# Self-attention's output projection by three float32r products of high and low parts, in a decoder layer on one core

## The reference

```
x = x + attn(layernorm(x))          # 16 heads of 128, one shared key/value head, rotary, causal
x = x + xattn(layernorm(x), ctx)    # 16 heads of 16 over 1500 context rows, layernorm of the output
x = x + ffn(layernorm(x))           # gated, with quantised activations and ternary weights
```

```
out = jnp.einsum('bhij,bjd->bhid', attn, v)
out = out.transpose(0, 2, 1, 3).reshape(b, n, h * dh)
return out @ Wo                     # (.., 2048) @ (2048, 256)
```

## Time and profile before

| | |
|---|---|
| median of 3 runs | 1477.72 us |
| the profiled execution's own time | 1479.29 us |
| its span, first to last instruction | 1477.5 us |
| PE busy | 1376.1 us, 93% |
| DVE busy | 1009.2 us, 68% |
| ACT busy | 717.3 us, 49% |
| POOL busy | 442.2 us, 30% |
| L643 records on PE | 512, 114.1 us busy |
| mean granted TensorE clock | 0.970 of full speed |

### The profile page before, as it was taken

The page is one execution under the profiler, slowest core; times in us unless marked ns, Lnnn a source line. Parts: engine busy times, 40 slices in busy tenths (PEclk is TensorE's granted clock), DMA queues, the critical chain, the costliest instruction groups (busy, mean ns, idle before and its releaser), DMA issues.

```text
span 1477.5 us, 55098 instructions
## 1 busy us (share of the span) xinstructions
PE 1376.1 (93%) x25094; PEld 1176.1 (80%) x25094; DVE 1009.2 (68%) x1786; ACT 717.3 (49%) x939; POOL 442.2 (30%) x394
## 2 busy tenths in 40 slices
PE   3899999999299999999999999999999999999983
PEld 3687777786278888888888888888888888888871
DVE  4666666765044686877778687876877777677765
ACT  1444454443155555464555555555555555555540
POOL 2332232231032323333333333332323233232400
PEclk8899999999689999999999999999999999999995
DMA  7000000000422211212121121211112121111100
GB/s 210 1 2 25 5 1 29 1 2 1 107 58 58 56 50 45 61 31 75 48 59 48 44 62 31 75 50 57 48 44 61 30 76 59 47 48 44 48 6 3
DMA packets 38809, 66.75 MB, mean 45 GB/s; under 512 B 3605, under 2 KB 36818, under 8 KB 38578
## 3 DMA queue, kind: packets, MB, share of 16 engines
q1 hardware_dynamic: 38578, 63.24, 14.7%
HBM read 61.40 MB, written 1.84 MB: 43 GB/s over the span
## 4 chain that ended last, share of the span: by engine, by line
PE 68%; DVE 3%; issue 1%; POOL 0%; POOLq 0%; DVEq 0%
PE proj_ps L1196 19%; PE proj_ps L1187 18%; PE score_ps L1214 13%; PE sum_ps L1234 12%; PE side_ps L1265 3%; PE side_ps L1251 2%; PE side_ps L1279 1%; PE side_ps L1272 1%; PE side_ps L1258 0%; DVE amax L1072 0%; DVE exps L1019 0%; DVE inv L1031 0%; POOL low L894 0%; DVE vals L1010 0%; DVE hidden L1104 0%
## 5 line engine op out<-in xcount | busy, mean ns | idle before, releaser
L954 ACT ACTIVATE exps<-score_ps 125x1792 f32<-125x1792 f32 x192 | 320.6, 1670 | 418.8 <-PE score_ps L1214 418.8
L894 POOL TENSOR_TENSOR low<-raw,high 128x500 fp32r<-128x500 f32 x192 | 293.6, 1537 | 645.1 <-PE proj_ps L1187 510.3
L1019 DVE TENSOR_SCALAR exps<-exps,top 125x896 f32<-125x896 f32 x384 | 288.1, 792 | 18.0 <-ACT exps L954 17.5
L1214 PE MATMUL score_ps<-spread,keys 32*125 32x112 f32 x6144 | 218.9, 279 | 0.9 <-ACT exps L954 0.9
L1234 PEld LDWEIGHTS sum_ps<-exps,vals 125*32 125x32 f32 x12288 | 163.5, 110 | 47.6 <-issue 33.9
L1214 PEld LDWEIGHTS score_ps<-spread,keys 32*125 32x125 f32 x6144 | 184.8, 183 | 16.3 <-ACT exps L954 1.0
L1010 DVE COPY vals<-proj_ps 125x512 f32<-125x512 f32 x192 | 128.3, 688 | 96.8 <-PE proj_ps L1196 96.3
L1234 PE MATMUL sum_ps<-exps,vals 125*32 125x56 f32 x12288 | 192.0, 215 | 0.1
L1196 PE MATMUL proj_ps<-w_h,high 128*125 128x256 f32 x768 | 165.0, 296 | 0.0
L1187 PE MATMUL proj_ps<-high,w_h 128*128 128x500 f32 x384 | 132.8, 427 | 25.4 <-POOL low L894 25.4
L946 ACT ACTIVATE keys<-proj_ps,b_k 128x500 f32<-128x500 f32 x192 | 130.0, 677 | 52.4 <-PE proj_ps L1187 48.0
(11 more groups left out here) (129 smaller groups left out, 1668.2 us busy)
## 6 DMA issues: line engine op xcount, KB each, us to landing
raw<-in_ctxT SPq DMA_DIRECT2D x96, 500.0 KB, 3.7
w_q<-in_attn_Wq SPq DMA_DIRECT2D x4, 512.0 KB, 6.7
w_o<-in_attn_Wo SPq DMA_DIRECT2D x1, 2048.0 KB, 19.9
out<-y_out SPq DMA_DIRECT2D x16, 112.0 KB, 2.0
rows<-in_x SPq DMA_DIRECT2D x1, 1568.0 KB, 14.8
w_raw<-in_ffn_gate_wT SPq DMA_DIRECT2D x1, 1024.0 KB, 8.6
w_raw<-in_ffn_val_wT SPq DMA_DIRECT2D x1, 1024.0 KB, 5.0
w_raw<-in_ffn_out_wT SPq DMA_DIRECT2D x1, 1024.0 KB, 5.8
```

Source lines behind the costliest of these rows:

```text
L894: nc.gpsimd.tensor_tensor(low[r][:, k, :], raw[ring][:, k, :], high[r][:, k, :].bitcast(F32), ALU.subtract).then_inc(low_ready, 1)
L954: nc.scalar.activation(exps[t % 2][:, :, :, :].rearrange("p h r n -> p r h n"), score_ps[0:TILE, :, 0:2 * QW].rearrange("p r (h n) -> p r ...
L1019: nc.vector.tensor_scalar(tile, tile, LIMIT_LO, top[:, n, at:at + 1], ALU.max, ALU.min)\
L1214: ins = nc.tensor.matmul(score_ps[0:TILE, r, to:to + HE * S], keys[c % 2][32 * r:32 * r + 32, k, (at + half) * TILE:(at + half + 1) * TILE ...
```

## The change

`Wo` and the heads' outputs are each split in two: a high part, which is the value rounded to float32r by a copy on ScalarE, and a low part, which is the value less its high part, computed on VectorE. The projection becomes three float32r matmuls per head (high with high, high with low, low with high) in place of one float32 matmul.

- `Wo` is split once, in pair 0: four ScalarE copies of 128x1024 after `exps(0)`, four VectorE subtractions of 128x1024 after the third rotary step.
- The heads' outputs are split in every pair: ScalarE's four copies write `outT_h` as float32r, and VectorE gets four new subtractions `out_low` of 128x448, each reading `out_ps` and `outT_h`. Two stand after the third rotary step and two after the fourth. `outT_ready`, for which `out_heads` and `out_rows` wait, is now counted by VectorE's subtractions and no longer by ScalarE's copies.
- `outT` had two buffers, `outT_h` and `outT_l` have one each.

```diff
@@ DVE
+            def out_low(p, k, b):
+                dve.wait_ge(outT_high, 2 * (2 * p + k) + b + 1)
+                nc.vector.tensor_tensor(outT_l[:, AU * k:AU * (k + 1), b * S:(b + 1) * S],
+                                        out_ps[:, b, 0:AU * S].rearrange("p (h s) -> p h s", s=S),
+                                        outT_h[:, AU * k:AU * (k + 1), b * S:(b + 1) * S].bitcast(F32),
+                                        ALU.subtract).then_inc(outT_ready, 1)
+            def out_weights(n):
+                dve.wait_ge(w_o_high, n + 1)
+                nc.vector.tensor_tensor(w_ol[:, 4 * n:4 * n + 4, :], w_o[:, 4 * n:4 * n + 4, :],
+                                        w_oh[:, 4 * n:4 * n + 4, :].bitcast(F32), ALU.subtract).then_inc(w_o_split, 1)
...
                 for name in more[2:3]:
                     rotary(name)
+                for n in range(4) if p == 0 else ():
+                    out_weights(n)
+                for b in range(2):
+                    out_low(p, 0, b)
                 if p:
                     norm2_rows(p - 1)
                 for name in more[3:4]:
                     rotary(name)
+                for b in range(2):
+                    out_low(p, 1, b)
@@ ACT
             def out_half(p, k, b):
                 act.wait_ge(pv_done, 2 * p + k + 1)
-                ins = nc.scalar.copy(outT[p % 2][:, AU * k:AU * (k + 1), b * S:(b + 1) * S],
-                                     out_ps[:, b, 0:AU * S].rearrange("p (h s) -> p h s", s=S))
-                ins.then_inc(outT_ready, 1)
+                nc.scalar.copy(outT_h[:, AU * k:AU * (k + 1), b * S:(b + 1) * S],
+                               out_ps[:, b, 0:AU * S].rearrange("p (h s) -> p h s", s=S)).then_inc(outT_high, 1)
+            def out_weights(n):
+                act.wait_ge(wo_in, 16)
+                nc.scalar.copy(w_oh[:, 4 * n:4 * n + 4, :], w_o[:, 4 * n:4 * n + 4, :]).then_inc(w_o_high, 1)
...
                 exps(p)
+                for n in range(4) if p == 0 else ():
+                    out_weights(n)
@@ PE
-                pe.wait_ge(wo_in, 16)
+                pe.wait_ge(w_o_split, 4)
                 pe.wait_ge(outT_ready, 4 * (p + 1))
                 for h in range(AH):
-                    ins = nc.tensor.matmul(to[0:ROWS, 0:D], outT[p % 2][:, h, :], w_o[:, h, :], start=(h == 0),
-                                           stop=(h == AH - 1))
+                    for n, (part, w) in enumerate(((outT_h, w_oh), (outT_h, w_ol), (outT_l, w_oh))):
+                        ins = nc.tensor.matmul(to[0:ROWS, 0:D], part[:, h, :], w[:, h, :], start=(h == 0 and n == 0),
+                                               stop=(h == AH - 1 and n == 2))
```

More of the change, by code:

```diff
@@ L47 @@
 TOTALS = (3, 7, 11)
+N_EARLY = 11 + 2 * HJ
 TILE = 125
@@ L110, in block_a @@
         w_o = sb("w_o", [P, AH, D])
+        w_oh = sb("w_oh", [P, AH, D], F32R)
+        w_ol = sb("w_ol", [P, AH, D], F32R)
         w_xq = sb("w_xq", [P, DC, D])
@@ L145, in block_a @@
         probsT = [sb(f"probsT{n}", [P, AU // 2, 2, S]) for n in range(2)]
-        outT = [sb(f"outT{n}", [P, AH, ROWS]) for n in range(2)]
+        outT_h = sb("outT_h", [P, AH, ROWS], F32R)
+        outT_l = sb("outT_l", [P, AH, ROWS], F32R)
         unit_ps = [ctx.enter_context(nc.psum_tensor(f"unit_ps{n}", [P, 512], F32)) for n in range(RING)]
@@ L187, in block_a @@
         outT_ready = sem("outT_ready")
+        outT_high = sem("outT_high")
+        w_o_high = sem("w_o_high")
+        w_o_split = sem("w_o_split")
         xq_ready = sem("xq_ready")
```

## The result

The changed kernel takes 1494.32 us (median of 4 runs, 1492.07 to 1496.05), the kernel before in the same job 1478.03 us (4 runs, 1477.56 to 1482.31). The ratio is 1.0103 (95% interval 1.0080 to 1.0126): slower by 16.3 us, where 11.4 us had been forecast. The profiled execution took 1493.92 us, 14.6 more than the profiled one of before.

What follows compares the result with a forecast made beforehand. TensorE, busy 93% of the span, was taken as the bound. Plain pairs +0.5, quantise pairs +4.1, pairs 14 and 15 +0.35, pair 0 +5.2 and +2.3, end -1.1 gave +11.4 us: 1489 us, range 1482 to 1495.

Steps and rivals of the forecast that it cites:

- the low clock: Pair 0, behind out_heads(0, 1): a new idle stretch of TensorE brings the clock down once, costing 2.3 us.
- Part 1: Output projection: 48 float32r matmuls at 0.118 us take 5.68 us against 6.79, saving 1.11 us, 16 times.
- Rival 2: Projection: float32r matmuls run at half a float32 record, 0.59 us more saved per projection; 1484 us, chance 12%, page's pace included.
- rival 5: Projection: each float32r product runs as two records like float32, +13.6 us each, some 1700 us; chance 1%.
- the estimate of 109 ns: Projection: the page's time per 256-column matmul, saving 1.55 us per projection; 1486 us, within Rival 2's chance of 12%.
- Part 2: out_heads(p, 1) waits for two VectorE subtractions, 1.18 us lost per pair; plain pairs +0.07 us each, +0.5 in all.
- Rival 1: Before out_heads(p, 1): subtractions are covered and all 16 savings arrive, -10.3 us, 1467 us; chance 5%.
- Part 3: Pairs not passing on the saving: +0.78 in 4, 8, 12, +0.59 in 2, 6, 10, +0.18 in 14 and 15.
- Part 4: Pair 0, split of the weights: out_heads(0, 1) starts 5.19 us later, and the low clock behind it costs 2.3 us.
- Rival 3: Pair 0 costs nothing because the weights' subtractions fit where VectorE is idle; +3.9 us, 1482 us, chance 8%.
- Part 5: End of block A: the last projection has nothing beside it, -1.1 us; its added wait is covered.
- Rival 4: Handovers cost up to 1.5 for 1.18 us in 15 pairs, low clock 1.2 more; +17, 1495 us, chance 9%.

Runs made afterwards that it cites:

- fourth experiment: Kernel before, float32 projection kept, with only the four subtractions per pair added, results unused but out_heads waiting for them; 1497.85 us, 1.0129 of the kernel before.
- second experiment: Changed kernel with three unused float32 matmuls ahead of out_heads(p, 1) in pairs 1 to 15; 1491.58 us, 1.0083 of the kernel before.
- third experiment: Changed kernel with VectorE's four weight subtractions in pair 0 moved from behind the third rotary step to behind normalise(0); 1492.94 us, 1.0101 of the kernel before.
- experiments 3, 4 and 5: The last: third experiment's kernel with the first output subtraction of pairs 0 to 13 moved inside the third rotary step; 1482.80 us, 1.0029 of the kernel before.
- ninth experiment: Changed kernel, weights split sooner, ScalarE's float32 copy freeing out_ps, low parts from it on VectorE (half 0) and GpSimd (half 1); 1466.79 us, 0.9915.
- eighth experiment: Third experiment's kernel without the low part of the outputs: no subtractions of them, 32 float32r matmuls; 1466.71 us, 0.9921 of the kernel before.
- sixth: Changed kernel with the edits of the second experiment and third experiment together; 1483.81 us, 1.0029 of the kernel before.
- the seventh: Changed kernel, weights split sooner, ScalarE's float32 copy freeing out_ps, VectorE's low parts behind the next pair's softmax, their products last; 1496.37 us, 1.0115.
- first experiment: Changed kernel without the four output subtractions per pair; third product takes the high parts again, still 48 matmuls; 1467.35 us, 0.9925 of the kernel before.

## Why the forecast fell 5 us short

The side and the mechanism were right, and the time lies within the range (1494.3; 1482 to 1495). Its working fell short by some 5 us of 16, and one of its terms, the low clock, was too small by more than that. In the two profiled executions, which are 14.6 us apart, the forecast of 11.4 misses by 3.2: low clock beyond the sum +6.9, everything else up to the start of block B -2.8, block B -0.9. The other 1.7 is how the medians lie to these two executions, and no trace shows it. By its own steps:

- **Part 1, the projection: right.** 5.66 us against 5.68. The pace of L1196 holds with 112 weight columns. Rival 2 (half a float32 record) falls with it, and so do rival 5 (768 records, one for each product) and the estimate of 109 ns worked out from the Trainium skill ("TensorE: Matmul & The Clock Gate", Back-to-back issue gap): 48 of them would have taken 5.2 us.
- **Part 2, the added wait: right.** Rival 1 (no wait) falls: out_heads(p, 1) waited in every pair. The fourth experiment isolates it: 1.18 us, as forecast from the neighbouring rotary row. In the changed kernel a plain pair comes out at -0.03 and not +0.07 us, since the saving is 1.13 and the wait eats all but that (pairs 3, 5, 11 and 13: -0.02, -0.04, -0.04, -0.03).
- **Part 3, the quantise pairs: right but for the last.** Pairs 2, 6 and 10 grew by 0.56, 0.68 and 0.56 (0.59 forecast), pair 4 by 0.77 (0.78), and pair 8, where the low clock lies over it, by 1.35 (0.75 in the second experiment). Pair 12 grew by 0.11 and not 0.78: I took it for a pair with a late VectorE, but no K and V rows are left to be normalised there. Pair 14 came out at -0.21 and not +0.18: its turn started 0.72 us sooner after the scores (9.15 for 9.87), where I had allowed 0.49.
- **Part 4, pair 0: right in sum.** out_heads(0, 1) started 23.02 us after the scores and not 17.65: 5.37 us, forecast 5.19. The four subtractions took 5.55 us in place of 4.56, but began 0.7 sooner after the scores, because the low clock ahead of them ended at 60.1 us and not at 62.2. The low clock behind them cost 0.85 in pair 0 and 1.13 in pair 1, 2.0 in all, forecast 2.3. Rival 3 falls: nothing hid them; even when the third experiment moved them, a wait of 2.63 us remained.
- **Part 5, the end: the term was right, and something lay over it.** Without the low clock 8.55 for 9.79, -1.24 us (forecast -1.1).
- **The mis-sized term is the low clock.** It stood in the sum once, 2.3 us for pair 0. The trace has it there and four times more: 2.9 + 2.3 + 2.0 = 7.2 us. Without these four the difference to the start of block B would be 15.5 - 7.2 = 8.3 us, so everything else together was forecast 3 us too high (start -0.8, pair 12, pairs 14 and 15, the plain pairs). The two misses lie on opposite sides, and that the total came out nearer than the low clock alone would have it is luck. I had read the earlier trace rows as if only a stretch of 4 or 5 us could bring it, though the trace of before has a fall, at 383.0 us, behind a shorter one:

```profile
381.67 0.38 PE L652 MATMUL unit_ps<-ident_a,normed 112*128 112x112 f32 x2 [2.66 <-DVE normed L383]
```

The added waits, which came to 1.1 to 1.9 us, I priced at their length alone.

Rival 4, more waiting, ends at 1495 us, beside the result, but most of its price is for another reason: the handovers were not dearer (fourth experiment), and the low clock cost 6.9 us more than the sum has, not 1.2. The list of what the profile would show is loose in one place: of the pairs 5 to 13 that it has about as long as before, part 3 means the odd ones.

**Which waits bring the low clock.** All executions with a wait for the subtractions before out_heads in pairs 1 to 15 (the changed kernel and experiments 3, 4 and 5), counted by the length of that wait:

```
idle before out_heads(p, 1)    waits    low clock at its end or within 2 us
0.69 to 0.75 us                  8       0
1.12 to 1.31 us                 32       0
1.41 us                          2       1
1.73 to 1.94 us                 18      11
```

In the kernel before the longest wait between 70 and 380 us is 1.17 us, and the clock never falls; the ninth experiment has no longer one than 1.32 from 90 to 369 us, and no fall. In the eighth, 2.35 to 3.00 us gave 5 of 6. In the second and sixth, where fillers leave at most 0.64 us of these waits, none of 30 gave a fall. So the quantise pairs pay twice: there TensorE comes to the wait sooner by the saving that VectorE can't follow, and the wait is 1.73 or 1.93 us and not 1.14. The last two pay twice as well, but for another reason: there TensorE waited 1.15 us for ScalarE's copy already in the kernel before, and the subtraction makes it 1.81, in the fourth experiment too. This also explains the fourth experiment, whose waits are all 1.14 in pairs 1 to 13, with no fall until the end of the second of two waits of 1.81 us, in pair 15. Against a bare rule by length stand the seventh, where seven waits of 1.6 us before the third product brought none, and the first and the eighth, where the clock falls in pair 15 about 2 us after a wait of only 1.15 us, with one of 1.06 between (the same two bring none in the kernel before and in the ninth). What else counts than the length stays open, and so does why one wait of 1.73 us is followed by a fall and the next isn't. Which ones are differs between executions (154 and 287 us in the third experiment, 200 in the changed kernel).

The Trainium skill ("TensorE: Matmul & The Clock Gate", A second HAM failure mode: psum-queue depth-cycling) tells of a kernel in which TensorE idles briefly and often between groups of matmuls, so that the clock goes to and fro and throughput is lost by its changes between the bursts. The traces here agree, with waits of 1.4 to 1.9 us once in a pair.

## What to carry to other kernels

Work that is cut from the busiest engine pays only where its releasers follow: read which instruction stands last before each of its waits, and put the new helper work (here a subtraction) anywhere but there. The same three products are 16 us slower than plain float32 with the subtractions on VectorE's path to TensorE, and 13 us faster with a ScalarE copy that frees PSUM and the subtractions where VectorE and GpSimd had been idle. Price a new wait on TensorE twice: its length, and, when it goes beyond the waits that the kernel already bears at full clock, the steps behind it at half the clock; compare the new waits with those in the trace of before (1.17 us here) to see whether you leave known ground. A wait within it is no guarantee, as pair 15 of the first experiment shows.

## What the runs showed of the hardware, beyond what was expected

- Of 20 waits on TensorE of 1.41 to 1.94 us, 12 were followed by a granted clock of 0.50. In the changed kernel the first three such stretches cost 1.3 to 1.5 us each in the steps behind them (pair 7 took 24.30 us, and 23.01 with the wait filled), and the last, from 384 to 391 us, 2.8.
- VectorE's subtraction of two SBUF sources slows beside GpSimd: one of the four weight pieces took 2148 ns, the others 1210 to 1218, while GpSimd's sines ran, themselves 1.74 us for 1.14. It is the one that starts second that gets longer: the sines had begun while the piece before was running, which kept its 1217. In the eighth experiment the rotary addition took 1.53 us for 0.62 beside the sines. The subtraction that reads PSUM never got longer (606 to 626 ns in 64), though seven of them ran beside GpSimd's products. The Trainium skill ("GPSIMD Engine Reference", Specifications) has GpSimd's way into SBUF shared with VectorE, in contention with instructions of two SBUF inputs: by that rule, the trace agrees.
- GpSimd subtracts 128x896 float32 from SBUF in 2.09 us, VectorE in 1.09 (ninth experiment).
